# Keys pass: transposes and key-value products take turns in two PSUM banks, and each batch's sums are folded on TensorE at the end of its keys pass

## What is computed

```python
q, k, v = xn @ wq, xn @ wk, xn @ wv                     # 16 heads of 32
def phi(u):                                             # 128 random features per head
    proj = u @ omega.T
    return exp(proj - 0.5*sum(u*u) - max(proj)) / sqrt(128) + 1e-6
pk, pq = phi(k * 32**-0.25), phi(q * 32**-0.25)
kv = einsum('bhsm,bhsk->bhmk', pk, v)                   # per batch and head, over 1024 rows
z  = sum(pk, axis=s)
out = (pq @ kv) / (pq @ z)
```

## Time and profile before

| | us |
|---|---|
| runs | 3785.38 (median), 3782.58, 3794.86 |
| the profiled execution | 3801.29 |
| span of its trace | 3799.5 |
| PE busy | 3564.6 (94%) |
| DVE, ACT, POOL busy | 2196.7, 1838.1, 1416.3 |

### The profile page before, as it was taken

One profiled execution on the slowest core, in us unless ns is written; L12 is line 12 of the kernel. 1 busy time (PEld: TensorE's weight loads), 2 busy tenths in 40 slices (PEclk: granted clock), 3 DMA queues, 4 the chain that ended last, 5 costly groups with the idle time before them and its releaser, 6 DMA issues. The chain is left out here.

```text
span 3799.5 us, 74203 instructions
## 1 busy us (share of the span) xinstructions
PE 3564.6 (94%) x27634; PEld 3134.4 (82%) x27634; DVE 2196.7 (58%) x3304; ACT 1838.1 (48%) x3944; POOL 1416.3 (37%) x954
## 2 busy tenths in 40 slices
PE   7989988898599999999999968999999999999998
PEld 6777777777488888888888857898898889998897
DVE  5777776677477777877878744333333333333332
ACT  5767766676355555655656534323223222333322
POOL 2544544454344444544445431222222222222222
PEclk9999999999699999999999988999999999999999
DMA  2221232212323232222332324111111111111111
GB/s 95 100 91 67 86 104 85 85 67 90 106 86 102 91 97 94 93 91 92 96 97 92 99 68 145 44 44 44 44 44 44 44 44 44 44 44 44 44 45 49
DMA packets 162443, 283.82 MB, mean 75 GB/s; under 512 B 23696, under 2 KB 52880, under 8 KB 161168
## 3 DMA queue, kind: packets, MB, share of 16 engines
q1 hardware_dynamic: 162192, 280.42, 21.8%
HBM read 166.08 MB, written 114.29 MB: 74 GB/s over the span
## 5 line engine op out<-in xcount | busy, mean ns | idle before, releaser
L1444 DVE TENSOR_TENSOR ffn_hT_lo<-ffn_hid,ffn_hT_hi 128x512 fp32r<-128x512 f32 x256 | 334.3, 1334 | 492.5 <-ACT ffn_hT_hi L1420 492.5
L96 PE MATMUL ffn_hidden<-ffn_yT_hi,ffn_wa_hi 128*128 128x256 f32 x2048 | 573.5, 280 | 11.9 <-DVE ffn_yT_lo L1440 11.9
L96 PE MATMUL ffn_hidden<-ffn_yT_hi,ffn_wa_lo 128*128 128x256 f32 x2048 | 573.6, 280 | 0.0
L96 PE MATMUL ffn_hidden<-ffn_yT_lo,ffn_wa_hi 128*128 128x256 f32 x2048 | 572.6, 280 | 0.0
L1411 ACT ACTIVATE ffn_hid<-ffn_hidden,ffn_bias 128x256 f32<-128x256 f32 x512 | 213.7, 468 | 669.0 <-PE ffn_hidden L96 646.3
L232 POOL TENSOR_TENSOR ffn_n_rstd<-ffn_n_base,ffn_n_power 128x2 f32<-128x2 f32 x32 | 22.5, 702 | 1072.6 <-DVE ffn_n_negmean L227 1072.6
L96 PE MATMUL ffn_result<-ffn_wb_hi,ffn_hT_hi 128*128 128x512 f32 x1024 | 412.0, 402 | 2.4 <-DVE ffn_hT_lo L1444 2.2
L96 PE MATMUL ffn_result<-ffn_wb_hi,ffn_hT_lo 128*128 128x512 f32 x1024 | 404.5, 395 | 0.0
L96 PE MATMUL ffn_result<-ffn_wb_lo,ffn_hT_hi 128*128 128x512 f32 x1024 | 404.2, 395 | 0.0
L96 PEld LDWEIGHTS ffn_hidden<-ffn_yT_hi,ffn_wa_hi 128*128 128x128 f32 x2048 | 384.9, 188 | 20.9 <-DVE ffn_yT_lo L1440 12.2
L96 PEld LDWEIGHTS ffn_hidden<-ffn_yT_lo,ffn_wa_hi 128*128 128x128 f32 x2048 | 385.2, 188 | 8.9
(11 more groups left out here) (229 smaller groups left out, 10112.3 us busy)
## 6 DMA issues: line engine op xcount, KB each, us to landing
attend_uq<-u_d SPq DMA_DIRECT2D x33, 512.0 KB, 3.6
ffn_y_in<-y_d SPq DMA_DIRECT2D x33, 512.0 KB, 3.7
keys_xin<-in_L_attn_x_dram SPq DMA_DIRECT2D x32, 512.0 KB, 5.6
xn_d<-keys_xn SPq DMA_DIRECT2D x32, 512.0 KB, 4.9
xT_d<-keys_xT_whole SPq DMA_DIRECT2D x32, 512.0 KB, 2.7
u_d<-keys_uq SPq DMA_DIRECT2D x32, 512.0 KB, 3.5
attend_xTf<-xT_d SPq DMA_DIRECT2D x32, 512.0 KB, 5.4
r_d<-attend_gate SPq DMA_DIRECT2D x32, 512.0 KB, 2.8
```

What stands on the lines that cost most here:

```text
L96: last = pe.matmul(out, stationary[a], moving[b], start=start and n == 0, stop=stop and n == len(TERMS) - 1)
L1444: dve.tensor_tensor(hT[n % HB].lo[:, :, :], hid[n % 2][:, :, :], f32(hT[n % HB].hi[:, :, :]), ALU.subtract).then_inc(h_ready[n % HB], 1)
```

## The change

Keys pass. The banks `turn` and `kv` become `aux0` and `aux1`. Transpose job n uses `aux[n]`, kv job n uses `aux[n % 2]`: kv 0 and kv 1 need not wait for an add, and kv 2 waits for the add of kv 0. The two transpose jobs of a kind now stand side by side. A new job `fold` at the end of each batch folds `kv_sum` and `z_sum` on PE (32 fp32 products, L645 and L650), ACT copies the results out (L506, L508), and SP stores 256 KB and 8 KB. The order tables of these two passes are new, but for POOL's in the keys pass. In `attend_pass` PE's jobs `z` and `kv` are gone; SP loads the folded sums into `kv_in` and `z_in` (`load_kv`), and one job `kv` on ACT and one on DVE (8 small instructions each) make `kvz` from SBUF.

```diff
-        turn = Bank(mem, ctx, "turn")
         feat = [Bank(mem, ctx, f"feat{j}") for j in range(HC)]
-        kv = Bank(mem, ctx, "kv")
+        aux = [Bank(mem, ctx, f"aux{n}") for n in range(2)]
...
         PE_BODY = [("proj", 0, 0), ("k", 0, 1), ("k", 1, 1), ("q", 0, 1), ("proj", 1, 0), ("turn_k", 0, 1),
-                   ("q", 1, 1), ("v", 0, 1), ("turn_k", 1, 1), ("kv", 0, 0), ("v", 1, 1), ("kv", 1, 0), ("kv", 2, 0),
-                   ("turn_x", 0, 2), ("kv", 3, 0), ("turn_x", 1, 2)]
+                   ("turn_k", 1, 1), ("q", 1, 1), ("v", 0, 1), ("kv", 0, 0), ("kv", 1, 0), ("v", 1, 1), ("kv", 2, 0),
+                   ("kv", 3, 0), ("fold", 0, 0), ("turn_x", 0, 2), ("turn_x", 1, 2)]
-        DVE_BODY = [("top", 0, 0), ("sq", 0, 1), ("pk", 0, 0), ("top", 1, 0), ("pk", 1, 0), ("turn_k", 0, 1),
-                    ("pk", 2, 0), ("pk", 3, 0), ("pk", 4, 0), ("stats", 0, 2), ("pk", 5, 0), ("kv", 0, 0),
-                    ("turn_k", 1, 1), ("pk", 6, 0), ("kv", 1, 0), ("pk", 7, 0), ("sq", 1, 1), ("kv", 2, 0),
-                    ("turn_x", 0, 2), ("v_out", 0, 1), ("kv", 3, 0), ("turn_x", 1, 2), ("v_out", 1, 1)]
+        DVE_BODY = [("top", 0, 0), ("stats", 0, 2), ("pk", 0, 0), ("top", 1, 0), ("pk", 1, 0), ("pk", 2, 0),
+                    ("turn_k", 0, 1), ("pk", 3, 0), ("pk", 4, 0), ("turn_k", 1, 1), ("pk", 5, 0), ("sq", 0, 1),
+                    ("kv", 0, 0), ("sq", 1, 1), ("pk", 6, 0), ("kv", 1, 0), ("pk", 7, 0), ("v_out", 0, 1),
+                    ("kv", 2, 0), ("kv", 3, 0), ("turn_x", 0, 2), ("turn_x", 1, 2), ("v_out", 1, 1)]
         POOL_BODY = [("z", 0, 0), ("z", 1, 0), ("z", 2, 0), ("z", 3, 0), ("stats", 0, 2), ("z", 4, 0),
                      ("whole", 0, 1), ("z", 5, 0), ("z", 6, 0), ("z", 7, 0)]
...
+                if job == "fold":
+                    act.wait_ge(folded, 2 * b + 1)
+                    wait(act, sums_stored, 32 * b)
+                    act.activation(kv_out[:, :], aux[0].t[:, :], ACT.Copy).then_inc(fold_out, 1)
+                    act.wait_ge(folded, 2 * b + 2)
+                    act.activation(z_out[:, :], aux[1].t[:, 0:2 * H].rearrange("p (h s) -> p h s", s=2)[:, :, 0], ACT.Copy)\
+                        .then_inc(fold_out, 1)
...
                 if job == "kv":
-                    wait(pe, kv.free, NC * g + n)
+                    if n >= 2:
+                        pe.wait_ge(kv_added, NC * g + n - 1)
+                    elif not (isinstance(g, int) and g == G - 1):
+                        pe.wait_ge(k_split, 2 * g + 3 + n)
...
+                if job == "fold":
+                    pe.wait_ge(fold_made, 4)
+                    pe.wait_ge(kv_added, NC * g + NC)
+                    for h in range(H):
+                        last = pe.matmul(aux[0].t[:, h * KD:(h + 1) * KD], kv_sum[:, h // HC, h % HC * M:(h % HC + 1) * M],
+                                         fold[:, h % 2, :], start=True, stop=True)
+                    last.then_inc(folded, 1)
+                    pe.wait_ge(z_added[1], NC * g + NC)
+                    for h in range(H):
+                        last = pe.matmul(aux[1].t[:, 2 * h:2 * h + 2], z_sum[:, h // HC, h % HC * M:(h % HC + 1) * M],
+                                         ones[:, :], start=True, stop=True)
+                    last.then_inc(folded, 1)
...
-        PE_BODY = [("max", 0, 0), ("z", 0, 0), ("num", 3, -1), ("k", 0, 0), ("max", 1, 0), ("z", 1, 0), ("k", 1, 0),
-                   ("r", 0, 0), ("below", 0, 0), ("feat", 0, 0), ("kv", 0, 0), ("r", 1, 0), ("turn_q", 0, 1),
+        PE_BODY = [("max", 0, 0), ("num", 3, -1), ("k", 0, 0), ("max", 1, 0), ("k", 1, 0), ("r", 0, 0),
+                   ("below", 0, 0), ("feat", 0, 0), ("r", 1, 0), ("turn_q", 0, 1), ("out", 0, 0), ("feat", 1, 0),
...
-                if job == "z":
-                    pe.wait_ge(z_loaded, 16 * (2 * b + n) + 16)
...
```

More of the change, by code:

```diff
@@ L331, in keys_pass @@
         ACT_BODY = [("k", 0, 1), ("exp", 0, 0), ("exp", 1, 0), ("exp", 2, 0), ("exp", 3, 0), ("hi", 0, 0),
[L332 to L335, removed]
+                    ("k", 1, 1), ("hi", 1, 0), ("q", 0, 1), ("turn_k", 0, 1), ("hi", 2, 0), ("turn_k", 1, 1),
@@ L336, in keys_pass @@
+                    ("hi", 3, 0), ("exp", 4, 0), ("hi", 4, 0), ("exp", 5, 0), ("hi", 5, 0), ("q", 1, 1),
+                    ("exp", 6, 0), ("hi", 6, 0), ("exp", 7, 0), ("hi", 7, 0), ("v_out", 0, 1), ("norm", 0, 2),
+                    ("fold", 0, 0), ("turn_x", 0, 2), ("turn_x", 1, 2), ("v_out", 1, 1)]
         POOL_BODY = [("z", 0, 0), ("z", 1, 0), ("z", 2, 0), ("z", 3, 0), ("stats", 0, 2), ("z", 4, 0),
                      ("whole", 0, 1), ("z", 5, 0), ("z", 6, 0), ("z", 7, 0)]
-        SP_BODY = [("x", 0, 2), ("whole", 0, 1), ("q", 1, 1), ("norm", 0, 2), ("sums", 0, 0)]
+        SP_BODY = [("x", 0, 2), ("q", 1, 1), ("whole", 0, 1), ("sums", 0, 0), ("norm", 0, 2)]
@@ L349, in body @@
                         continue
-                    if job == "sums" and i != GB - 1:
+                    if job in ("fold", "sums") and i != GB - 1:
                         continue
@@ L386, in do @@
                 if job == "sums":
[L387 to L393, removed]
+                    wait_alone(sp, fold_out, 2 * b + 2, sp_passed)
+                    sp.dma_start(kv_d[b], kv_out[:, :]).then_inc(sums_stored, 16)
+                    sp.dma_start(z_d[b], z_out[:, :]).then_inc(sums_stored, 16)
             run(sp, do, SP_BODY)
@@ L404, in _ @@
             norm.init(pool)
+            pool.memset(ones[:, :], 1.0).then_inc(fold_made, 1)
+            pool.memset(fold[:, :, :], 0.0).then_inc(fold_made, 1)
+            pool.wait_ge(ident_made, 2)
+            pool.wait_ge(fold_made, 2)
+            for a in range(2):
+                half = slice(a * 2 * KD, (a + 1) * 2 * KD)
+                at = a * 2 * KD
+                pool.tensor_tensor(fold[half, a, :], ident[half, at:at + KD], ident[half, at + KD:at + 2 * KD], ALU.add)\
+                    .then_inc(fold_made, 1)
+            pool.wait_ge(fold_made, 4)
             def do(job, n, g, b, i):
@@ L409, in do @@
                 if job == "whole":
-                    pool.wait_ge(turn.free, 4 * g + 2)
+                    pool.wait_ge(x_split, 2 * g + 2)
                     wait(pool, xT_stored, 16 * g)
@@ L439, in do @@
                     act.wait_ge(norm.ready, g + 1)
-                    wait(act, turn.full, 4 * g - 2)
+                    wait(act, x_turned, 2 * g)
                     wait(act, xn_stored, 16 * g)
@@ L456, in do @@
                     act.wait_ge(dense[n].full, 3 * g + 1)
-                    wait(act, turn.full, 4 * g)
+                    wait(act, k_turned, 2 * g)
                     wait(act, sq_ready[n], g)
@@ L468, in do @@
                         wait(act, feat[j].full, TG * g)
[L469 to L470 removed]
+                    act.wait_ge(k_turned, 2 * g + n + 1)
+                    act.activation(kT.hi[:, 2 * n:2 * n + 2, :], halves(aux[n]), ACT.Copy).then_inc(kT_hi, 1)
                 if job == "exp":
@@ L538, in do @@
                 if job == "kv":
+                    bank = aux[n % 2]
                     if i == 0 and n == 0:
[L540 to L542 removed]
+                        wait(dve, folded, 2 * b)
+                    dve.wait_ge(kv_full, NC * g + n + 1)
+                    wait(dve, kv_added, NC * (g - 1) + n + 1)
                     if i == 0:
[L544 removed]
+                        dve.tensor_copy(kv_sum[:, n, :], bank.t[:, :]).then_inc(kv_added, 1)
                     else:
[L546 removed]
+                        dve.tensor_tensor(kv_sum[:, n, :], bank.t[:, :], kv_sum[:, n, :], ALU.add).then_inc(kv_added, 1)
             run(dve, do, DVE_BODY)
@@ L574, in do @@
                         pe.wait_ge(w_split, (k + 1) * (n_w // 3))
-                    pe.wait_ge(turn.free, 4 * g + 2)
+                    pe.wait_ge(x_split, 2 * g + 2)
                     wait(pe, dense[n].free, 3 * g + k)
@@ L581, in do @@
                 if job == "proj":
-                    pe.wait_ge(turn.free, 4 * g + 4)
+                    pe.wait_ge(k_split, 2 * g + 2)
                     wait(pe, e_ready[1 - n], NC * g + NC if n == 1 else NC * g)
@@ new lines, in attend_pass @@
+        DVE_BODY = [("top", 0, 0), ("top", 1, 0), ("recip", 0, -1), ("below", 0, 0), ("mix", 0, 1), ("kv", 0, 0),
+                    ("exp", 0, 0), ("o", 0, -1), ("out", 0, 0), ("sq", 0, 1), ("turn_q", 0, 1), ("mix", 1, 1),
+                    ("out", 1, 0), ("hi", 1, 0), ("wo", 0, -1), ("turn_q", 1, 1), ("wo", 1, -1), ("sq", 1, 1),
+                    ("stats", 0, -1)]
+        ACT_BODY = [("num", 3, -1), ("norm", 0, -2), ("k", 0, 0), ("k", 1, 0), ("below", 0, 0), ("kv", 0, 0),
+                    ("r", 0, 0), ("exp", 0, 0), ("sq", 0, 1), ("mix", 0, 1), ("r", 1, 0), ("turn_q", 0, 1),
+                    ("oT", 0, -1), ("num", 0, 0), ("exp", 1, 0), ("num", 1, 0), ("hi", 1, 0), ("turn_q", 1, 1),
+                    ("sq", 1, 1), ("mix", 1, 1), ("num", 2, 0)]
```

196 lines of the change are left out of this document (77 added, 119 removed).

## The result

| | before | changed |
|---|---|---|
| median of the runs, us | 3787.49 (3782.58 to 3794.86, 4 runs) | 3930.97 (3929.42 to 3934.24, 4 runs) |
| span of the trace, us | 3799.5 | 3927.5 |
| start of the attend pass (SP's first DMA) | 983.79 | 1164.31 |
| start of the feed-forward pass (PE's first transpose) | 2286.6 | 2413.4 |

The change makes the kernel 3.8% slower: ratio 1.0378, 95% interval 1.0359 to 1.0398. I had forecast slower by 89 us, 3874; it is slower by 143 us by the medians, which lies outside my range (to 3915). Between the two traces it is 128 us; the profiled execution of before was itself some 14 us above its median. By pass: keys +180.5, attend -53.7, feed-forward +1.2.

A forecast was written before the change was run, and what follows sets the result against it. PE, busy 94% of the span, was taken to set the time. Terms +33 +15 +55 +28 +8 -2 -61 +13 = +89 on 3785.4 gave 3874 us, range 3762 to 3915 (the main case's own 3830 to 3915).

The forecast's parts named there:

- the mechanism of the held `pk`: Keys groups: early `stats` frees POOL, whose `z` 4 and `whole` hold the fourth and fifth `pk`; kv 0 waits 2.2 us.
- The step as a whole: Two banks in steady keys groups: 3.4 us of new waits against 2.27 saved, +1.1 us per group, +33 in 30 groups.
- Clock in steady groups: Keys pass: the new 2.2 us PE wait lowers the clock in three groups in ten, +15 us, between 0 and 51.
- the full 51: Keys pass: upper bound for lowered clock after the new PE wait, 30 groups at 1.7 us each.
- the clock drops everywhere: Rival: every keys group (51) and each batch end (60) pays for lowered clock, 3942 us; chance 0.10.
- Clock and fold at batch ends: Keys pass, seven batch ends: folding products 7.9 us each, +55, and lowered clock 4 each, +28.
- The 4: Keys pass: us added per batch end for lowered clock around the folding products, +28 in all, between 0 and 60.
- Attend pass: Folding products leave PE, -61 us; `kvz` made from SBUF on DVE beside POOL, +13; the pass -48.
- the step of the waits: Steady keys groups: PE waits for held `pk` outweigh the add waits saved by two banks, +33 us.
- POOL does not hold the fifth `pk`: Rival, keys groups: kv 0 starts on time, two banks gain 57 us, no clock loss in groups; 3769 us, chance 0.20.

The follow-up runs named there:

- Before, with stats early: The kernel before the change with one job moved: DVE does `stats` behind the first `top`; 3867.22 us.
- the kernel with whole first: The changed kernel with one POOL job moved: `whole` runs first in each keys group, ahead of `z` 0; 3821.66 us.
- the pair of runs with whole first: POOL's `whole` moved first in the kernel before (3772.40 us), and in the two banks and new order with folding left in the attend pass (3768.92 us).

## Why the prediction was wrong

**Direction, and the mechanism of the held `pk`: right.** It was argued from two rows of before that a `pk` is held to the end of the running POOL instruction, that `stats` early on DVE would move this onto the fourth and fifth `pk`, and that kv 0 would wait 2.2 us, kv 1 0.74 and the transposes 0.46. Measured: 2.26, 0.52, 0.33. The step as a whole was small, though: +1.1 us per group without clock was forecast, and it is 2.8 less 1.3 of clock, about 1.5, some 10 us more in the kernel. The forecast had set idle times of PE (2.2) against a loss counted by starts (2.27). By starts kv 0 costs 2.4: its first product comes 2.65 us after the last one of v 0, where these products are 0.23 apart.

**The step that failed: "Clock in steady groups", +15.** I gave the wait three chances in ten of lowering the clock, because it was "a little shorter than any that I see followed by a drop" (2.7 us). It is lowered behind every such wait of the changed kernel's steady groups, for 1.3 us each: some 39 us in 30 groups. The reason that I gave was a misreading of the trace of before. It has four turns of the loop in the attend pass at which PE sits idle for 2.19 to 2.41 us, and the clock is down directly behind three of them:

```profile
1475.02 0.33 PE L1140 MATMUL attend_feat<-attend_omegaT_hi,attend_qT_hi 32*128 32x128 f32 x4 [2.27 <-issue]
1629.32 0.48 PE L1140 MATMUL attend_feat<-attend_omegaT_hi,attend_qT_hi 32*128 32x128 f32 x4 [2.19 <-issue]
1785.57 0.33 PE L1140 MATMUL attend_feat<-attend_omegaT_hi,attend_qT_hi 32*128 32x128 f32 x4 [2.41 <-issue]
```

```profile
1475.02:1477.02 2.00, 2.00 (x48) 2.00 (x48) 0.00 (x0) 0.00 (x0) 1.44 (x3) 0.64 0.08 20
1629.32:1631.32 2.00, 2.00 (x40) 2.00 (x40) 0.00 (x0) 0.00 (x0) 1.51 (x3) 0.50 0.07 21
1785.57:1787.57 2.00, 2.00 (x48) 2.00 (x48) 0.00 (x0) 0.00 (x0) 1.18 (x3) 0.66 0.07 23
```

At the head of the keys pass a wait of 2.08 us (to 36.30) has a clock of 1.00 behind it and one of 1.66 (to 44.50) a clock of 0.61. So rows of the same length were there, most of them with a drop; they asked for more than three in ten, and the full 51 belonged in the range. The length alone doesn't settle it either: the changed kernel has a turn of 2.19 us (to 1487.11) with the clock at 1.00 for the next 6 us, and the run "Before, with stats early" goes either way at 2.60. What else decides stays open. My rival "the clock drops everywhere", at one chance in ten, gave 3942 for 3931 measured.

**Clock and fold at batch ends: near at one end, short in the sum.** 7.9 + 4 = 11.9 us per batch was forecast; at the end looked at it is 19.4 - 7.4 = 12.0, and 1.5 in the group behind. But of the seven ends before, three had cost nothing over a group (28.2, 28.1 and 27.9 us), and all seven cost now: by the starts of POOL's L232 the ends and the groups behind them add 107 us in all; 83 were forecast. The 4 stood for a lowered clock around the fold, as in the window at 1168.50; the products alone lose 4.9 to it, since they take 12.2 us and not 7.3. That forecast and measurement meet at this end is in part luck, as the other ends of before show.

**Attend pass**: -48 forecast, -53.7 measured. **Sum by passes**: keys +137 forecast, +180.5 measured, 43 more: the clock in the steady groups is 24 of it, the step of the waits 10, the batch ends 24, and what is left, -15, was not broken down (head and last batch are in it). By experiments: the two banks and the new order without the fold cost 70 us (3864 against 3794), where 46 were forecast (33 + 15 - 2); moving the fold costs 67 on top, where 43 were.

The rival "POOL does not hold the fifth `pk`" is what the kernel with whole first comes near to. It takes 3822 there, not 3769: with `whole` out of the way the gain is 0.7 us per group, not 1.9 (36 of the 53 us), and the batch ends cost more; the earlier trace rows misled me about the first. Their waits were put down to the bank's adds, but a third of them was the adds' own lateness behind `pk` jobs that POOL held. The sentence of the Trainium skill ("TensorE: Matmul & The Clock Gate", section "HAM oscillation — how this bites in real kernels") that a second PSUM buffer "gave no further gain", which I set against those rows, agrees with the pair of runs with whole first: 3772.4 with one bank for the kv jobs, 3768.9 with two and the new order. The exclusive lock of the Trainium skill ("SBUF — State Buffer", section "Who interferes with whom") agrees with the rows of the changed kernel, where the fourth and fifth `pk` end 0.55 us after `z` 4 and `whole`.

## What to carry to other kernels

When a job is moved, follow what it releases on other engines, not only what stood around it: here a cheap DVE job moved forward let POOL's next work start 5 us earlier, into the very instructions that TensorE needed next. Put POOL's long two-input work where DVE reads PSUM or reduces, before looking for more banks. Price a wait on TensorE with the clock it may cost: look in the trace for every idle time of about that length, whatever it waits for, loop turns too, and see what the clock does behind each. Where they go both ways, carry the full price in the range. Price many tiny products in a row from a stretch of them at the lower clock: here 64 took 12.2 us, where their count at full clock gave 7.3.
